# Moving one of 39 fields of each job from VectorE to ScalarE and GpSimd in a fused recommendation tower

## What is computed

```python
e = jnp.stack([tbl_f[ids[:, f]] for f in range(39)], axis=1)      # [512, 39, 16]
prev = x = e
for k in range(3):                                                 # three layers, 128 units each
    z = jnp.einsum('bmd,bhd->bdmh', x, prev).reshape(b, D, m * h)
    t = jnp.einsum('bdc,co->bdo', z, ws[k]) + bs[k]
    t = jnp.transpose(t, (0, 2, 1))
    t = t / jnp.sqrt(jnp.sum(t * t, axis=(-2, -1), keepdims=True))
    logit.append(t)
    prev = t
z = jnp.sum(jnp.concatenate(logit, axis=1), axis=-1)               # [512, 384]
h = relu(concat([z, dense_ctx]) @ W_top1 + b_top1)
h = relu(h @ W_top2 + b_top2)
y = h @ W_top3
```

## Time and profile before

| | us |
|---|---|
| median of 3 runs (1060.4 to 1062.07) | 1061.88 |
| the profiled execution | 1062.48 |
| its span, first to last instruction | 1060.8 |
| PE busy | 1028.2 (97%) |
| DVE busy | 983.6 (93%) |
| POOL busy | 865.9 (82%) |
| ACT busy | 791.3 (75%) |
| granted clock of PE | full throughout |

### The profile page before, as it was taken

The page is one execution under the profiler, slowest core; times in us unless marked ns, Lnnn a source line. Parts: engine busy times, 40 slices in busy tenths (PEclk is TensorE's granted clock), DMA queues, the critical chain, the costliest instruction groups (busy, mean ns, idle before and its releaser), DMA issues.

```text
span 1060.8 us, 17970 instructions
## 1 busy us (share of the span) xinstructions
PE 1028.2 (97%) x4320; PEld 782.4 (74%) x4320; DVE 983.6 (93%) x3344; ACT 791.3 (75%) x2655; POOL 865.9 (82%) x729
## 2 busy tenths in 40 slices
PE   2999999999999999999999999999999999999998
PEld 0477777878777787877778787777878777788884
DVE  2589999999999999999999999999999999999993
ACT  3476877868788786868778687777868778788872
POOL 6777988889898888988888898888889888577770
PEclk9999999999999999999999999999999999999999
DMA  5650030302303030120303012030301203000000
GB/s 188 129 143 12 3 88 3 89 2 52 96 4 88 3 87 4 21 71 2 89 3 87 5 28 64 3 89 2 85 7 17 74 3 89 1 1 1 2 1 1
DMA packets 75892, 46.10 MB, mean 43 GB/s; under 512 B 55689, under 2 KB 58633, under 8 KB 75658
## 3 DMA queue, kind: packets, MB, share of 16 engines
q1 hardware_dynamic: 68487, 38.59, 15.2%
q10 hardware_dynamic: 2179, 5.07, 1.4%
q0 software_dynamic: 5120, 1.29, 1.4%
HBM read 42.99 MB, written 1.94 MB: 42 GB/s over the span
## 4 chain that ended last, share of the span: by engine, by line
PE 48%; POOL 19%; DVE 18%; issue 9%; ACT 5%; DMA 1%; POOLq 0%; DVEq 0%; SPq 0%; ACTq 0%
POOL sums L432 14%; DVE sums L946 12%; PE acc L778 8%; PE bank_d L722 7%; PE bank_d L723 6%; PE bank_d L724 6%; PE bank_a L724 6%; PE bank_a L722 6%; PE bank_a L723 6%; POOL gathered L415 5%; ACT scaled L560 4%; DVE bank_d L946 2%; DVE sums L965 1%; ACT sums L560 1%; PE turned L799 1%
## 5 line engine op out<-in xcount | busy, mean ns | idle before, releaser
L432 POOL TENSOR_TENSOR sums<-sums,scaled 128x512 f32<-128x512 f32 (+1 forms) x512 | 645.1, 1262 | 133.4 <-ACT scaled L560 97.4
L946 DVE SCALAR_TENSOR_TENSOR sums<-bank_d,x_col,sums 128x128 f32<-128x128 f32 x2304 | 654.2, 339 | 29.3 <-PE bank_d L724 20.2
L560 ACT ACTIVATE scaled<-bank_a,x_col 128x128 f32<-128x128 f32 x1920 | 551.5, 385 | 139.8 <-PE bank_a L724 132.7
L722 PE MATMUL bank_d<-w_hi,prev_lo 128*128 128x512 f32 x640 | 288.0, 450 | 6.2 <-DVE sums L965 4.7
L722 PE MATMUL bank_a<-w_hi,prev_lo 128*128 128x512 f32 (+1 forms) x640 | 263.9, 412 | 2.6 <-issue 1.3
L724 PE MATMUL bank_d<-w_hi,prev_hi 128*128 128x512 f32 x640 | 252.5, 394 | 0.0
L723 PE MATMUL bank_d<-w_lo,prev_hi 128*128 128x512 f32 x640 | 252.1, 394 | 0.0
L724 PE MATMUL bank_a<-w_hi,prev_hi 128*128 128x512 f32 (+1 forms) x640 | 245.3, 383 | 0.0
L723 PE MATMUL bank_a<-w_lo,prev_hi 128*128 128x512 f32 (+1 forms) x640 | 245.1, 383 | 0.0
L560 ACT ACTIVATE sums<-bank_a,x_col 128x128 f32<-128x128 f32 x512 | 146.1, 369 | 76.8 <-PE bank_a L724 75.9
L415 POOL DMA_INDIRECT gathered<-in_table,idx x160 | 177.2, 1108 | 28.5 <-issue 18.3
(11 more groups left out here) (84 smaller groups left out, 528.2 us busy)
## 6 DMA issues: line engine op xcount, KB each, us to landing
x_pairs<-x_scratch SPq DMA_DIRECT2D x135, 156.0 KB
x_pairs<-x_scratch SPq DMA_DIRECT2D x96, 78.0 KB
gathered<-in_table,idx POOLq DMA_INDIRECT x160
x_sq<-x_scratch SPq DMA_DIRECT2D x32, 64.0 KB
x_pairs<-x_scratch SPq DMA_DIRECT2D x92, 22.0 KB
x_scratch<-gathered SPq DMA_DIRECT2D x16, 72.0 KB
w_raw<-in_w ACTq DMA_DIRECT2D x1, 1024.0 KB, 5.1
w_raw<-in_w ACTq DMA_DIRECT2D x1, 896.0 KB
```

The lines of the kernel that those rows point to most:

```text
L432: nc.gpsimd.tensor_tensor(out=sums[:, n % SUMS, 0:w, :], in0=sums[:, n % SUMS, 0:w, :], in1=scaled[:, a - 1, 0:w, :], op=ALU.add).then_inc ...
L560: op = nc.scalar.activation(to[:, i, :], bank_a[at % A_RING][:, i * UNITS:(i + 1) * UNITS], ACT.Copy, scale=x_of(c, q, a * PER_BANK + i))
L722: nc.tensor.matmul(to, lo, w_h, start=True, stop=False)
L946: nc.vector.scalar_tensor_tensor(out=taken(n, u) if u in LEFT else total, in0=taken(n, u), scalar=x_of(c, q, A_FIELDS + u), in1=total, op0 ...
```

## The change

ScalarE's fifth bank gets four fields in place of three, and VectorE's fifth bank three in place of four. ACT has 20 L560 per job instead of 19, POOL's fourth add is 128x512 instead of 128x384, DVE has 19 L946 instead of 20. The matmuls of ScalarE's fifth bank go from 384 to 512 columns and those of VectorE's fifth from 512 to 384. `LEFT` goes from (17, 18) to (16, 17) and `TOTAL` from slot 0 to slot 3, both computed from `D_FIELDS`. The second line changes one place of DVE's order: with 19 fields there is no field 19, so the sums of the item (0, 1) come one field earlier.

```diff
@@ -44,7 +44,7 @@
 A_BANKS = 5
 BANKS = -(-FIELDS // PER_BANK)
 D_BANKS = BANKS - A_BANKS
-A_FIELDS = A_BANKS * PER_BANK - 1
+A_FIELDS = A_BANKS * PER_BANK
 D_FIELDS = FIELDS - A_FIELDS
 ADDS = A_BANKS - 1
 
@@ -75,7 +75,7 @@
-FINISHES = [(0, 0, None, None), (0, 1, (0, 3), (0, 16)), (1, 0, (step_at(1, 0), 3), (step_at(1, 1), 0))]
+FINISHES = [(0, 0, None, None), (0, 1, (0, 3), (0, 15)), (1, 0, (step_at(1, 0), 3), (step_at(1, 1), 0))]
```

## The result

The changed kernel takes 1068.61 us (median of 4 runs, 1068.36 to 1068.70). The kernel before has 1061.97 with the runs made beside it. The ratio is 1.0066 (95% interval 1.0048 to 1.0083): slower by 0.7%, 6.6 us. The profiled execution took 1068.7 us, its span is 1067.0.

The account below looks back on a forecast made before the run. PE was taken as the bound, DVE close behind. Thirteen steps at 0.67 us gave +8.7, less 1.2 saved elsewhere: +7.5 in all, a forecast of 1069.4 us (chance 0.45), range 1059 to 1076.

Parts of the forecast that it names:

- The bound and its chain: Each step: PE bounds, its stop reached through PE, ACT, some 30 us of POOL, 16 us of DVE; steps become 62.9 us.
- PE and ACT at nothing: PE's moved columns and ACT's additional L560 per job priced at 0; 0.17 us if someone waits on PE's place.
- the anchor: POOL's wait for ACT at 480.65, where the counted stretch begins; claimed to just hold, with 0.02 us of slack left.
- POOL's term, 0.93 us: Four wider adds between 480.65 and 510.25 cost 1.06 us, less 0.13 of slack; DVE starts the seventh job 0.93 later.
- the 0.13 of slack that I had found: POOL's idle at 491.83, where it waited for ACT: of 0.27 us, 0.13 or so was taken as slack.
- The bound of 1.06: Upper bound on DVE's later start at the seventh job: 1.06 us if the 0.13 at 491.83 is no slack.
- The multiply tied to POOL: Pair multiply L914 ends a fixed time after POOL's add, so only one of DVE's 0.26 us savings counts: 0.67 a step.
- rival 2: L914 gets in one POOL instruction earlier, behind L437: 0.12 us a step, +0.4 in all, 1062.3 us; chance 0.12.
- The exclusive port: Skill rule cited for rival 2: the first to start holds the shared port; alone it puts the multiply behind L437.
- The rest, -1.2 us: DVE's savings where POOL is not in the chain: first steps 0.5, last jobs 0.5, steps 14 and 15 0.2.
- Rival 3: DVE's relief reaches PE, given 0.4 us more POOL slack: a step gains 0.52, 1053.9 us; chance 0.14.
- Rival 4: Delays build up: the anchor gives way and no saving counts, 13 x 0.93 = +12.1, about 1074 us; chance 0.08.

Follow-up runs that it names:

- e_narrow_add: Changed kernel with POOL's last add of each job kept at 128x384, the fourth field's product left out of the sum; 1055.53 us, 0.9946 of before.
- e_low_later: Changed kernel with layer 1's L437 two places later in POOL's order, behind the seventh job's last add, its high part on ACT moving along; 1057.02 us.
- e_before_act: Kernel before with only the 128 additional ACT instructions, their fourth slot never read, POOL's add still 128x384; 1059.99 us, 0.9982 of before.
- e_before_wide: Kernel before with the additional ACT instructions and POOL's last add at 128x512, DVE keeping 20 fields; 1076.19 us, 1.0135 of before.
- e_pairs_8: Changed kernel with each step's first pair multiply behind field 8 of the eighth job, not field 12; 1066.23 us, 1.0054 of before.
- e_pairs_11: Changed kernel with each step's first pair multiply behind field 11 of the eighth job, not field 12; 1065.75 us, 1.0035 of before.
- e_before_low_later: Kernel before, complete, with only layer 1's L437 two places later in POOL's order; 1051.21 us, 0.9888 of before.

## Why the prediction was right

**The bound and its chain.** Steps were to take 62.9 us and nine of the twelve take 62.8 to 62.9. The time was to be 1069.4 and is 1068.6. The chain through POOL is shown from two sides: with POOL's columns taken back the loss turns into a gain (e_narrow_add), and with POOL's order changed and nothing else it does too (e_low_later).

**PE and ACT at nothing.** Right for ACT: its instructions alone cost nothing (e_before_act). For PE the 0.17 us that I had named in case someone waits did come through. One row of before and one of after, ACT's first bank of the step's third job:

```profile
477.22 1.14 ACT L560 ACTIVATE sums<-bank_a,x_col 128x128 f32<-128x128 f32 x4 [0.62 <-PE bank_a L724]
```

```profile
543.12 1.14 ACT L560 ACTIVATE sums<-bank_a,x_col 128x128 f32<-128x128 f32 x4 [0.35 <-PE bank_a L724]
```

Counted from the step's start, with PE's stops in the first job taken off (0.87 and 0.65 us), the first starts at 477.22 - 460.55 - 0.87 = 15.80 and the second at 543.12 - 526.50 - 0.65 = 15.97, 0.17 us later. In e_before_act, where PE's columns are those of before, this bank has no such delay. ACT then works almost without idle up to the bank that the anchor's add waits for, and that add is 0.18 us later (19.41 against 19.23).

**POOL's term, 0.93 us.** A little too small, and as near as it is because its errors partly cancel. In the same count DVE's first field of the seventh job is 1.08 us later than before: (577.16 - 526.50 - 0.65) against (510.35 - 460.55 - 0.87). e_before_wide gives 1.12. The parts: the anchor's add is 0.18 later by PE's columns, and the gather at 551.28 behind it 0.25. The first wide add makes that 0.52, at 553.72 (before 487.47). Then POOL catches up 0.33, more than the 0.13 of slack that I had found: at 559.20 (before 493.28) it is only 0.19 behind. It used up the idle in front of the adds that follow L405, and a part of the 0.27 at 491.83. The three wide adds after that cost 0.88, not 0.80, and the last one ends 1.07 late. The bound of 1.06 was the better value, but not for its reason, since there was slack.

**The multiply tied to POOL.** Right in outcome: it ended at 589.99, 1.08 us behind the add of 587.63, and one field of DVE's two was lost in waiting. The reason that I gave was wrong. I argued from the multiply at 476.78 that it waits out an add which follows without idle, so that L437's end would be no way in. e_pairs_8, e_pairs_11 and e_before_low_later show it go in exactly there. By my sum it would have come 0.13 us ahead of L437's end, and rival 2 would have been the result. It came 0.05 us behind (587.72 against 586.38 + 1.29), because in the count above the multiply moved by 0.82 and not by 0.67, and L437 by 0.90 and not by 0.93. That the forecast came and not rival 2 was therefore luck, by 0.05 us, and rival 2 deserved more than 0.12. e_pairs_11 shows what it would have been worth: 0.4 us a step.

**The exclusive port.** The rule of the Trainium skill under rival 2 ("SBUF — State Buffer", "Who interferes with whom": who starts first holds it to the end) fits the multiplies beside L437 and the adds better than my reading did. Beside gathers the recorded starts alone do not give the order, below. The other rule, that such a multiply does not stall a gather, is half right: a gather that runs when the multiply comes mostly takes its 0.97 us (e_pairs_11), one that begins beside it mostly takes 1.77 as before.

**The rest, -1.2 us.** Half of it came. From step 14 to the end, for which I had 0.7, the changed kernel is 0.9 us shorter: 0.26 in step 14, 0.2 in step 15, 0.4 behind it. The 0.5 of the first steps did not come: up to step 1 nothing is gained but the sooner start of the loop, which varies by several us between traces, and step 1 is 0.9 us longer, where the sum's thirteen steps have 0.67 for it.

**Rival 3** (DVE's relief reaches PE) did not come. With POOL's order mended a step falls to 61.9 us (e_low_later), below the 62.24 of before; but the kernel before in the same order has 61.27, so even then the moved field is no gain. **Rival 4** did not come: POOL still waits for ACT at the anchor, with 0.05 us, so the delay does not build up from step to step.

## What to carry to other kernels

An engine at 89% of the span can be the one that a step waits for, if its idle time lies elsewhere than the stretch that feeds the release. Before a piece of work is moved to it, follow the releases back from the bottleneck's stops and count what the move puts in front of each one. Here the order of two instructions on the receiving engine was worth more than the piece: 1.1% by moving one 1.3 us instruction behind the add that others wait for, part of it through the multiply that then got in sooner, against the 0.7% that moving the field cost.

## What the runs showed of the hardware

A multiply of VectorE with both inputs in SBUF and an add or subtraction of GpSimd shut each other out, and 0.1 to 0.3 us in the arrival decide which goes first: a swing of 2.2 to 1.2 us for the one and 1.3 to 2.3 for the other. Beside adds the order follows the recorded starts: the multiply goes in 0.1 us ahead of L437's end (e_before_low_later) and waits out the next add 0.05 behind it (the changed kernel).

Beside a gather with an add right behind it, the recorded starts do not give the order. The third multiply arrived 0.46 us before the gather's end and waited out the add (2.60 us, at 476.78); in e_before_act it arrived 0.46 before as well and went in at once. What differs is when ACT had the add's data ready. ACT's row for that add, first in the kernel before, then in e_before_act with the multiply:

```profile
475.71 0.89 ACT L560 ACTIVATE scaled<-bank_a,x_col 128x128 f32<-128x128 f32 x3 [0.94 <-PE bank_a L724]
```

```profile
538.72 1.14 ACT L561 ACTIVATE scaled<-bank_a,x_col 128x128 f32<-128x128 f32 x4 [0.94 <-PE bank_a L725]
539.79 1.21 DVE L915 TENSOR_TENSOR z<-x_pairs 117x1024 f32<-117x1024 f32 x1
```

ACT ended 0.18 us ahead of the multiply's start in the one (476.60) and 0.07 behind it in the other (539.86). The 13 traces have 147 third multiplies that start while such a gather runs. The 98 that went first started at most 0.12 us after ACT had ended, the 49 that waited out the add 0.12 to 0.31 us after. So the add seems to claim its turn when its data is ready, though the gather in front of it still runs; that reading is inferred from the order. The second multiply of a step comes when ACT is long done (0.78 us or more). It goes first if it starts up to 0.24 us behind the gather's start (55 of them) and waits from 0.38 on (56), but for eleven, all in step 5, where the gather itself took 1.25 to 2.65 us. What differs in that step is open.
